# The start of a three-layer CIN kernel on one Trainium2 core: gathers, loads and the first chunks of block 0 in another order

## The reference

```python
x0 = prev = inputs                                   # (2048, 39, 16)
for i, f in enumerate([128, 128, 128]):
    h = prev.shape[1]                                # 39, then 64, 64
    Wr = Ws[i].reshape(h, M, f)
    z = relu(einsum('bhk,bmk,hmf->bfk', prev, x0, Wr) + bs[i][None, :, None])
    results.append(z[:, :f // 2]); prev = z[:, f // 2:]
pooled = sum(concatenate(results, axis=1), axis=-1)
return pooled @ W_lin                                # (2048, 1)
```

## Time and profile before

| | |
|---|---|
| Time, median of 3 runs | 2015.1 us (2013.05 to 2015.74) |
| The profiled execution: time, span | 2011.91 us, 2010.1 us |
| PE busy | 1998.9 us (99%) |
| DVE busy | 1791.3 us (89%) |
| ACT busy | 520.2 us (26%) |
| DMA | 307.11 MB, mean 153 GB/s |

### The profile page before, as it was taken

How to read it: one execution, slowest core, us unless ns; L and a number is a source line. 1 busy time by engine, 2 the same in 40 slices (tenths; PEclk the granted TensorE clock), 3 DMA queues, 4 the chain that set the end, 5 groups by cost and what they waited for, 6 DMA issues and landing times.

```text
span 2010.1 us, 19878 instructions
## 1 busy us (share of the span) xinstructions
PE 1998.9 (99%) x6328; PEld 803.8 (40%) x6328; DVE 1791.3 (89%) x1184; ACT 520.2 (26%) x485; POOL 2.2 (0%) x7
## 2 busy tenths in 40 slices
PE   8999999999999999999999999999999999999999
PEld 3344333444333443334433344433444333443343
DVE  7988998888988889888898888898888988889888
ACT  2331133321233212333113332133321233311332
POOL 0000000000000000000000000000000000000000
PEclk9999999999999999999999999999999999999999
DMA  7967976668766678666786667876678866678610
GB/s 186 214 139 155 195 151 143 149 145 187 168 145 144 148 170 186 140 149 144 156 194 146 147 143 152 187 166 147 140 151 171 180 150 141 148 156 194 148 36 1
DMA packets 98877, 307.11 MB, mean 153 GB/s; under 512 B 19281, under 2 KB 20178, under 8 KB 98860
## 3 DMA queue, kind: packets, MB, share of 16 engines
q1 hardware_dynamic: 98012, 306.69, 70.3%
q10 hardware_dynamic: 848, 0.20, 0.1%
HBM read 306.81 MB, written 0.01 MB: 153 GB/s over the span
## 4 chain that ended last, share of the span: by engine, by line
PE 97%; DVE 2%; DMA 1%; issue 0%; ACTq 0%; SPq 0%; ACT 0%; DVEq 0%
PE acc L465 68%; PE acc L535 25%; PE acc L459 3%; DVE prod L296 1%; PE acc L544 1%; DMA x_seed<-x 0%; DVE x_bc L258 0%; DVE prod L302 0%; DMA prod<-x 0%; PE acc L477 0%; DVE x_rot L268 0%; SPq L203 0%; PE acc_y L589 0%; ACTq L646 0%; PE acc L595 0%
## 5 line engine op out<-in xcount | busy, mean ns | idle before, releaser
L296 DVE TENSOR_TENSOR prod<-prev,x_bc 128x2048 f32<-128x2048 f32 x512 | 1138.1, 2282 | 4.2 <-PE acc L465 4.2
L465 PE MATMUL acc<-prod,w_sb 128*128 128x512 f32 x2432 | 1052.5, 594 | 0.2 <-DVE prod L296 0.2
L465 PEld LDWEIGHTS acc<-prod,w_sb 128*128 128x128 f32 x2432 | 460.0, 190 | 592.3 <-issue 562.9
L535 PE MATMUL acc<-prod,w_sb 128*64 128x512 f32 x2432 | 530.0, 594 | 1.3 <-DVE prod L296 1.3
L605 ACT ACTIVATE prev<-acc,bias 64x1024 f32<-64x1024 f32 x128 | 142.0, 1109 | 1310.5 <-PE acc L465 1290.2
L465 PE MATMUL acc<-x_rot,w_sb 117*128 117x512 f32 (+1 forms) x768 | 335.9, 593 | 3.3 <-DVE x_rot L268 3.3
L535 PEld LDWEIGHTS acc<-prod,w_sb 128*64 128x64 f32 x2432 | 171.4, 137 | 356.0 <-issue 302.1
L610 ACT ACTIVATE prev<-acc,bias 32x1024 f32<-32x1024 f32 x256 | 283.2, 1106 | 4.0
L302 DVE TENSOR_TENSOR prod<-prev,x_bc 128x1024 f32<-128x1024 f32 x192 | 228.7, 1217 | 1.5
L465 PEld LDWEIGHTS acc<-x_rot,w_sb 117*128 117x128 f32 (+1 forms) x768 | 145.5, 190 | 188.9 <-issue 188.1
L268 DVE TENSOR_TENSOR x_rot<-x_rot,x_rep 124x1024 f32<-124x1024 f32 (+1 forms) x188 | 216.0, 1217 | 0.0
(11 more groups left out here) (39 smaller groups left out, 100.6 us busy)
## 6 DMA issues: line engine op xcount, KB each, us to landing
x_bc<-x SPq DMA_DIRECT2D x310, 256.0 KB, 10.8
x_bc<-x SPq DMA_DIRECT2D x155, 512.0 KB, 18.7
x_rot<-x SPq DMA_DIRECT2D x186, 312.0 KB
x_rot<-x SPq DMA_DIRECT2D x192, 156.0 KB
x_bc<-x SPq DMA_DIRECT2D x124, 128.0 KB, 6.7
x_rep<-x SPq DMA_DIRECT2D x62, 192.0 KB
x_rep_s<-x SPq DMA_DIRECT2D x64, 128.0 KB, 22.3
x_rot_s<-x SPq DMA_DIRECT2D x64, 128.0 KB, 22.4
```

The source lines that it names most:

```text
L296: mul = nc.vector.tensor_tensor(prod[:, s:s + w, :], twice, x_bc[:, u, t:t + w, :], ALU.mult)
L465: mm = nc.tensor.matmul(acc[:, h, :], w, rhs[:, BANK * h:BANK * h + BANK], start=start, stop=stop)
L535: mm = nc.tensor.matmul(acc2[HALF * h:HALF * h + HALF, u, :], w2_sb[:, ORDER[pos], :], prod[:, pos % RING, BANK * h:BANK * h + BANK], star ...
```

## The change

Only block 0's start is touched; the loops over the other blocks are as they were.

- PE: a half-wide dummy matmul (256 columns) more ahead; all five gathers in a row, in five PSUM places (a new two-bank tile `acc_s` takes gather 2); one dummy matmul in place of three behind layer 0.
- Loads: ACT issues `x_seed` before its copy of `x_rep`, as four loads; behind the copy only the bias b0. The other six small loads are issued by SP behind w1, and so are tiles T2 and T1 of block 0, now loaded (1 MB) and not shuffled. w1 comes in two parts, not three.
- DVE: tiles 0, 1, 2, 3 are shuffled between the last products of layer 0; tile 4 and the others later, between products of layer 1.
- Eviction of layer 0: ACT takes columns 0 to 511 of prev10, DVE columns 512 to 1023 (`tensor_scalar`). The turned copies stay on ACT.
- Layer 1 begins with chunk 0 in two halves of 512 columns, each as soon as its half of prev10 is there; the narrow T1 chunk comes last.

```diff
-    W1_PARTS = [(CH - 1, CH), (0, 5), (5, CH - 1)]
-    ORDER_FIRST = [CH - 1, *range(5), *range(T + 2, T + 6), T + 1, T, 5, 6, T + 6, T + 7, 7, 8, T + 8, T + 9]
+    W1_PARTS = [(0, 5), (5, CH)]
+    ORDER_FIRST = [0, 1, 2, 3, T + 1, T + 2, T + 3, T + 4, 4, 5, T + 5, T + 6, 6, 7, T + 7, T + 8, 8, T, T + 9, CH - 1]
+    RUNS_FIRST = [(0, 1), (1, 1), *((p, 2) for p in range(2, 18, 2)), (18, 1), (19, 1)]
...
+        made_in = [acc2, acc_s, acc1, acc2]
...
+            load_bc_last(0, 0, first_bc_loaded)
+            sp.dma_start(bias[:, 1:2], b1).then_inc(small_loaded, 16)
...
+                seeds = {3: (4,), 4: (5,), 6: (6, 7), 7: (8,)}
+                spread = {1: 2, 2: 4, 5: 6, 7: 8, 9: 9}
+                for h in range(NH):
+                    cols = slice(BANK * h, BANK * h + BANK)
+                    if h == 0:
+                        dve.wait_ge(seed_spread, 1)
+                    dve.wait_ge(prev_half[h], 1)
+                    nc.vector.tensor_tensor(prod[:, 0, cols], prev[0][0][:, cols], x_bc[:, 0, 0, cols],
+                                            ALU.mult).then_inc([half_ready, prod_ready][h], 1)
...
-            dve.wait_ge(seed_loaded, 16 * 2 * QPT)
-            seed(T1)
-            product0_made(3, acc1)
+            product0_made(3, made_in[3])
             dve.wait_ge(rep_loaded, 16)
             for c in range(2):
                 dve.wait_ge(rot_loaded[c], 16 * ROT_LOADS[c])
                 product0(c, x_rot[0:ROWS0[c], c, :])
+                for t in ((0, 1), (2,))[c]:
+                    seed(t)
             product_split(0)
-            for t in range(5):
-                seed(t)
+            seed(3)
+            dve.wait_ge(bias0_loaded, 16)
+            dve.wait_ge(acc0_full, 1)
+            for g in range(2):
+                op = nc.vector.tensor_scalar(prev[0][0][HALF * g:HALF * g + HALF, BANK:NB], acc0[HALF:P, 1, :],
+                                             bias[HALF:P, 0:1], 0.0, ALU.add, ALU.max)
+            op.then_inc(prev_half[1], 1)
...
             keep_warm(2)
+            keep_warm(1, BANK // 2)
             layer0_first()
-            keep_warm(3)
-            layer1(0, 0, ahead=False, order=ORDER_FIRST, parts=W1_PARTS)
+            keep_warm(1)
+            layer1_first()
...
+            def evacuate0_first():
+                act.wait_ge(acc0_full, 1)
+                for g in range(2):
+                    op = nc.scalar.activation(prev[0][0][HALF * g:HALF * g + HALF, 0:BANK], acc0[HALF:P, 0, :],
+                                              ACT.Relu, bias=bias[HALF:P, 0:1])
+                op.then_inc(prev_half[0], 1)
+                act.sem_inc(prev_ready[0], 1)
+                act.wait_ge(prev_half[1], 1)
+                spread_turned(prev[0], acc0, 0)
...
-            act.wait_ge(rep_made, 1)
-            nc.scalar.activation(x_rep[0:DPC * M, :], acc1[0:DPC * M, :, :].rearrange("p h n -> p (h n)"),
-                                 ACT.Copy).then_inc(rep_copied, 1)
             act.wait_ge(seed_cleared, 1)
             for q in range(QPT):
                 base = x[0, q:q + 1, :]
                 rows = bass.AP(tensor=base.tensor, offset=base.offset, ap=[[QPT * NB, T], [1, NB]])
                 act.dma_start(x_seed[QUAD * q:QUAD * q + T, :], rows).then_inc(seed_loaded, 16)
-                act.dma_start(x_seed[QUAD * q + T:QUAD * q + T + 3, :], x[0, QPT * T:M, :]).then_inc(seed_loaded, 16)
-            act.dma_start(bias[:, 0:1], b0).then_inc(small_loaded, 16)
...
```

More of the change, by code:

```diff
@@ L55, in cin_kernel @@
     LAST = NBLK - 1
-    assert BATCH == P // QUAD * BANK
+    assert BATCH == P // QUAD * BANK and len(RUNS_FIRST) == NR
     with ExitStack() as ctx:
@@ L127, in cin_kernel @@
         seed_loaded = sem("seed_loaded")
+        bias0_loaded = sem("bias0_loaded")
+        first_bc_loaded = [sem(f"first_bc_loaded{n}") for n in range(2)]
         seed_spread = sem("seed_spread")
@@ L133, in cin_kernel @@
         prod_ready = sem("prod_ready")
+        half_ready = sem("half_ready")
+        prev_half = [sem(f"prev_half{h}") for h in range(NH)]
         chunk_used = sem("chunk_used")
@@ L194, in load_bc @@
                         sp.dma_start(x_bc[QUAD * q:QUAD * q + QUAD, u, t0:t1, :], src).then_inc(bc_loaded[u][g], 16)
[L195 to L199, removed]
+                load_bc_last(i, u, (bc_loaded[u][BC_T2], bc_loaded[u][BC_T1]))
             for g in range(2):
@@ L254, in seed @@
             def seed(t):
[L256 to L259, removed]
+                if t == 0:
+                    dve.wait_ge(seed_loaded, 16 * QPT)
+                nc.vector.stream_shuffle(x_bc[:, 0, t, :], x_seed[:], [t] * QUAD).then_inc(seed_spread, 1)
             def product_split(i):
@@ L283, in products0, with product @@
                         product0(c, x_rot[0:ROWS0[c], c, :])
-            def product(layer, n, u, phase=0, order=ORDER):
-                pos, w = RUNS[n]
+            def product(layer, n, u, phase=0, order=ORDER, runs=RUNS):
+                pos, w = runs[n]
                 a, t = CHUNKS[order[pos]]
@@ L305, in products1_seeded @@
             def products1_seeded():
-                spread = {0: 1, 1: 2, 2: 4, 3: 6, 7: 8, 8: 10, 10: 12}
-                late = {6: (T2,), 7: (5, 6), 9: (7, 8)}
-                for n, (pos, w) in enumerate(RUNS):
+                seeds = {3: (4,), 4: (5,), 6: (6, 7), 7: (8,)}
[7 more added lines that the diff above has]
+                                            ALU.mult).then_inc([half_ready, prod_ready][h], 1)
+                for n in range(1, NR):
+                    pos, w = RUNS_FIRST[n]
                     if n in spread:
                         dve.wait_ge(seed_spread, spread[n])
-                    if pos in (0, 6):
-                        dve.wait_ge(prev_ready[0], 1 if pos == 0 else 2)
+                    if n == 3:
+                        dve.wait_ge(prev_ready[0], 2)
+                    if n in (9, 11):
+                        dve.wait_ge(first_bc_loaded[0 if n == 9 else 1], 32 if n == 9 else 16)
                     dve.wait_ge(chunk_used, pos + w)
-                    product(1, n, 0, order=ORDER_FIRST)
-                    for t in late.get(n, ()):
+                    product(1, n, 0, order=ORDER_FIRST, runs=RUNS_FIRST)
+                    for t in seeds.get(n, ()):
                         seed(t)
@@ L381, in _ @@
             dve.wait_ge(rep_copied, 1)
-            product0_made(0, spare)
-            product0_made(1, acc1)
+            for n in range(3):
+                product0_made(n, made_in[n])
             dve.wait_ge(w0_loaded, 64)
```

83 lines of the change are left out of this document (58 added, 25 removed).

## The result

| | before | after |
|---|---|---|
| Time, median of 20 runs each | 2014.51 us (2011.98 to 2015.74) | 2011.74 us (2007.27 to 2013.4) |
| Ratio after / before | | 0.9984, 95% interval 0.9977 to 0.9990 |
| Profiled execution: time, span | 2011.91, 2010.1 | 2011.94, 2010.0 |
| Granted clock, mean of the profiled span | 1.000 | 0.998 |

The kernel became faster by 2.8 us, 0.16% (0.10 to 0.23%). The forecast was 2007.9 us, a gain of 7.2: right in sign, 2.6 times too large, and the measured 2011.74 lies 0.1 us beyond the upper end of the range (2004.5 to 2011.6). What the prediction called "faster" was a gain of over 4.0 us, to which it gave 0.85; a gain of 2.8 is what it called "same", at 0.12. The two profiled executions differ by 0.1 us in span, and that pair shows best what happened: nearly the whole forecast gain was made by 60 us, and given back at 90.

A forecast was written before the change was run, and what follows sets the result against it. PE, busy 99% of the span, was taken as the bound, with gains only from idle or dummy-filled time. Gains of 5.4 us in layer 0 and 1.8 in layer 1 made 7.2: 2015.1 to 2007.9 us, range 2004.5 to 2011.6.

The forecast's parts named there:

- Mark A: End of block 0's layer 0 matmuls on PE: 28.32 us before, forecast 22.9, a gain of 5.4 us.
- Mark A, the gathers: PE's side of layer 0: five gathers in a row from 5.95, 1.05 us each, chunk 2 at 11.3.
- I take 11.3, a rise within gather 0: PE's clock reaches 2.4 GHz during the first gather, so the five gathers end at 11.3 us, not 12.7.
- the pause: PE's 0.54 us idle between starting dummies and gathers; the half-wide dummy was to close it, bringing the clock rise earlier.
- Mark A, DVE's cover: In layer 0, DVE has products ready 0.8 us or more before PE asks, so PE sets the layer's end.
- a hole opens in layer 0's chunks: Sign of a wrong prediction: PE idles between chunks of layer 0, where no hole was forecast.
- From A to B: End of layer 0's matmuls to end of block 0's layer 1: 36.8 us against 38.6, gain 1.8.
- B: End of layer 1 of block 0 on PE: 66.91 us before, forecast 59.7.
- What lies behind B: After block 0's layer 1: PE has the same work without notable holes, delayed loads cost nothing.
- PE waits for DVE after A + 6.3: Sign of a wrong prediction: PE waits for DVE later than 6.3 us after layer 0 ends; no such wait forecast.
- The clock's rival: Third rival: clock falls in PE's 1.5 us idle before layer 1; gain only 2.9 us, 2012.2; chance 0.07.
- The base: Profiled execution before, 2011.91 us, on which the sum was made and carried as a difference to the 2015.1 median.

The follow-up runs named there:

- e6: Changed kernel without the half-wide dummy matmul ahead of the gathers; ratio to the kernel before 0.9984.
- e9: The kernel before, unedited, profiled a second time in one execution; span 2011.5 us.
- e4: Changed kernel with block 2's four narrow loads issued by ACT on its own queue instead of SP's; ratio to the kernel before 0.9973.
- e3: Changed kernel plus one 0.5 MB load behind T1 on SP's queue, into a tile nothing reads; ratio to the kernel before 0.9998.
- e12: Changed kernel with T1 of block 0 shuffled again, late, so 0.5 MB less on SP's queue; ratio to the kernel before 0.9974.
- e1: Changed kernel with T2 and T1 of block 0 shuffled again, so 1 MB less of loads; ratio to the kernel before 0.9977.
- e7: Changed kernel with four dummy matmuls on PE ahead of block 1's layer 1; ratio to the kernel before 0.9976.
- e8: Changed kernel with T1 shuffled again, late, and block 2's narrow loads and the six small loads on ACT's queue; 2005.94 us, ratio to the kernel before 0.9964.
- e11: e8 with the x_seed loads behind ACT's copy of x_rep, as in the kernel before; ratio to the kernel before 0.9974.
- e5: Changed kernel with the four x_seed loads behind ACT's copy of x_rep, as in the kernel before; ratio to the kernel before 0.9968.
- e10: Changed kernel unedited, timed and profiled again on another chip; ratio to the kernel before 0.9981.

## Why the prediction was right or wrong

- **Mark A, the gathers: near in number, wrong in reason.** Chunk 2 was forecast at 11.3 and came at 10.50. The five gathers began where they should (5.96, forecast 5.95) and took 4.54, 0.9 each; 1.05 was read off a gather between two chunks, and is too long for gathers in a row. (the earlier trace rows show four passes to a gather, 0.43 each, and not two of 0.86; the price of the half-wide dummy, a matmul at the slow level, came out right all the same.) The step "I take 11.3, a rise within gather 0, because the pause is the only difference" fails in its reason: e6 without the half dummy and e9, the kernel before, have the pause and the early rise. It was an accident of the one profiled execution that the rise came at 10.1 there: in the other 13 traces, with a pause or without, gathers 0 and 1 took 1.98 to 2.70 us together. The page of the Trainium skill that was cited (TensorE: Matmul & The Clock Gate, What's actually happening) says "the default state is throttled, and activity releases the throttle", and also that the moment depends on the phase in which the kernel starts. The traces agree with this second part, which the prediction left out: fast gathers at 5.69 in one execution of a kernel, slow ones until about 10 in another.
- **Mark A, DVE's cover: too optimistic.** It was called thin and was: 22.9 forecast, 23.47 measured. From a chunk 2 that came 0.8 us early the forecast's own sum gives 22.1, so 1.4 us were lost in between, and that A is off by only 0.6 is in part luck. The loads of chunks 0 and 1, which weren't priced, kept DVE for 0.95 and 0.70 us, and PE for 1.18. `x_seed` made no wait, as said. In e4, the same program up to there, A was at 22.61. That "a hole opens in layer 0's chunks" was one of the prediction's own signs of being wrong, and one of 1.18 us did.
- **From A to B: right.** 36.74 us (60.21 - 23.47) against 36.8 forecast. PE began at A + 2.60 (forecast 2.35), and resumed at A + 6.45 (6.3). The two tensor_scalars took 1.53 together, 0.77 each with what lies between; 0.65 was taken. The row below is the changed kernel's. The rule of the Trainium skill that was cited on PSUM operands (VectorE: DVE Perf Modes, Why PSUM operands drop a tier) agrees with it, as the 0.41 of the doubled rate isn't there.

```profile
23.68 1.53 DVE L429 TENSOR_SCALAR prev<-acc,bias 64x512 f32<-64x512 f32 x2
```

- **What lies behind B: wrong, and this is the step that failed.** "What they delay, w2 and block 1's loads, has as long. I cost these at nothing", and "PE behind B has the same work and no holes to speak of". Time to landing was taken from an unburdened stretch (11.3 us) and compared with 30 us of slack for the load itself; what had to be compared is the whole of SP's queue with PE's need: 1 MB more (about 5 us at 200 GB/s), asked for by a PE that is 6.7 us earlier. The margin of the narrow load was about 9 us before (82 against 91); the sum of the two is over 11. It should have been the fifth rival: the wait turns up at block 2's narrow load, 60 us behind the place that was changed. Measured were a need 6.3 us sooner (85.1 against 91.4), a landing 8 us later (90 against 82), a hole of 3.86 us and 2.7 for the clock; the forecast had 0 for all of it, and "PE waits for DVE after A + 6.3" was its own sign of being wrong. What shows the cause: the narrow load's 24.3 us to landing against 12.3 by the other queue (e4), the doses in time (e3, e12, e1), and the order of the holes by bytes moved less bytes put in front.
- **The clock's rival was seen in the wrong place.** It was given 0.07 for PE's pause before layer 1, where it never fell. It fell behind the hole at 88, at a price of 2.7 us, and e7 shows that the price is one of its own. That this rival's number, 2.9 us of gain, is so near to the measured 2.8 is luck: it had no hole of 3.86 us and another place for the fall.
- **The base: not a typical execution.** The profiled execution of before had a hole of 3.03 us and no fall; most of the timed ones do worse (e9: A at 29.66). Against e9's trace the change is 8.0 us ahead at B (60.21 against 68.18), not 6.7, and 1.5 at the end (spans 2010.0 and 2011.5). The difference of medians, 2.8, is a mixture of executions with and without falls on both sides, and no single pair of traces gives it.

What stays open: what sets the rate of the queue. From 30 to 60 us it moved 192 and 190 GB/s in the changed kernel and 213 and 208 before, at much the same share of busy engines; but e6, with the same loads, moved 212 and 197, and e8 and e11, which differ in the place of x_seed alone, 187 and 185 against 220 and 216. So it isn't shown that the change slowed the queue. The last of these windows, before and after:

```profile
45.00:60.00 15.00, 15.00 (x37) 6.64 (x36) 14.90 (x14) 0.00 (x0) 0.00 (x0) 1.00 1.04 208
```
```profile
45.00:60.00 15.00, 15.00 (x42) 6.44 (x44) 14.20 (x13) 0.00 (x0) 0.00 (x0) 1.00 1.03 190
```

## What to carry to other kernels

When a change makes the consumer earlier and adds bytes to a queue, add the two up and compare them with the margin of the load that is asked for first behind that queue, however far off it is: bytes in front of it, over the rate of a full queue, against the need. Where single traces disagree with a dose, count the bytes that the queue had moved by then before the theory is given up. An idle stretch of the DMA engines that gets filled is no proof of a lead: here the bytes moved by 60 us stayed the same. And take a profile of before more than once before its holes are priced: the same hole cost 3.0 us in one execution and 6.2 with its slower clock in another.

## What was not expected of the hardware

- The four narrow loads, 0.5 MB, landed 24.3 us after issue in the full queue of SP (after), and 9.7 to 12.3 us after issue on ACT's queue at the same time of the kernel (e4). The place in a queue with little in it was worth 12 us here.
- The rise of PE's clock at the start came between about 4 and 10 us in kernels that begin alike: six dummy passes took 3.85 us in e5 and 4.64 in e7, against 4.31 in the changed kernel. Only the kernel before, in one of its two traces, was slow until 10.
- A hole of PE sometimes lets the clock fall and sometimes not: it fell after 2.21 (e11), 3.19 (e10), 3.86 (after), 4.22 (e3) and 4.47 us (e9), and not after 2.63 (e4), 2.76 (e12) and 3.03 us (the kernel before). The falls in these traces cost 1.6 (e11) to 2.8 us (e10) on top of the hole.
- Between traces of kernels with the same loads in SP's queue, what the DMA engines had moved by 60 us differs by 0.9 MB (11.43 MB in the changed kernel, 12.33 in e5).
